# Graph network layer with a residual norm: the first edge layer's bias and maximum on VectorE, more rows fetched outside GpSimd

## What is computed

```python
ef = relu(edge_attr @ We1 + be1) @ We2 + be2          # edge_attr: 106250 x 64
ef = ef * sigmoid(edge_weight[:, None] @ Wt + bt)
msg = relu(concatenate([x[src], ef], axis=1) @ Wn1 + bn1) @ Wn2 + bn2
out = segment_sum(msg, dst, num_segments=6250)
return layernorm(x + (out + x))
```

## Time and profile before

| | us |
|---|---|
| median of 3 runs | 1045.51 (1045.18 to 1046.26) |
| the profiled execution, its own time | 1047.54 |
| its span in the trace | 1045.7 |
| PE busy | 850.5 (81%) |
| PEld busy | 613.4 (59%) |
| DVE busy | 650.3 (62%) |
| ACT busy | 492.0 (47%) |
| POOL busy | 777.1 (74%) |
| mean granted TensorE clock | 0.956 of full |

### The profile page before, as it was taken

The page is one execution under the profiler, slowest core; times in us unless marked ns, Lnnn a source line. Parts: engine busy times, 40 slices in busy tenths (PEclk is TensorE's granted clock), DMA queues, the critical chain, the costliest instruction groups (busy, mean ns, idle before and its releaser), DMA issues.

```text
span 1045.7 us, 21663 instructions
## 1 busy us (share of the span) xinstructions
PE 850.5 (81%) x5035; PEld 613.4 (59%) x5036; DVE 650.3 (62%) x1688; ACT 492.0 (47%) x668; POOL 777.1 (74%) x826
## 2 busy tenths in 40 slices
PE   6989998888788779787887777778888797887884
PEld 6766666566566556455555555555555565664653
DVE  4767775755665655656467466566566566566566
ACT  5565454445355445344445445444444444544432
POOL 7776777777777777777777777777777777777773
PEclk9999999999999998999899999998998998999997
DMA  8984555565554544554455445454544554554311
GB/s 231 284 232 121 146 146 147 145 155 144 145 154 123 153 141 126 134 154 138 123 145 154 137 124 156 116 145 130 158 128 124 145 145 127 143 144 145 84 53 49
DMA packets 158963, 148.85 MB, mean 142 GB/s; under 512 B 123255, under 2 KB 127414, under 8 KB 158822
## 3 DMA queue, kind: packets, MB, share of 16 engines
q1 hardware_dynamic: 128550, 89.86, 30.8%
q0 software_dynamic: 26144, 53.60, 19.5%
q10 hardware_dynamic: 4128, 3.87, 1.1%
HBM read 140.85 MB, written 6.40 MB: 141 GB/s over the span
## 4 chain that ended last, share of the span: by engine, by line
POOL 53%; issue 24%; PE 8%; DMA 7%; DVE 5%; ACT 2%; SPq 1%; DVEq 0%; ACTq 0%; POOLq 0%
POOL gathered L532 53%; DMA gathered<-node_table,src_e 5%; PE psS L852 2%; DVE h L1173 2%; PE psM L894 2%; DMA x_sb<-in_x 1%; PE psH L907 1%; PE psE L919 1%; ACT tw L693 1%; ACT h L625 0%; DVE onehot L1179 0%; SPq L431 0%; SPq L425 0%; PE psS L837 0%; DVE gathered L1047 0%
## 5 line engine op out<-in xcount | busy, mean ns | idle before, releaser
L532 POOL DMA_INDIRECT gathered<-node_table,src_e x785 | 745.2, 949 | 241.4 <-issue 233.9
L698 ACT ACTIVATE h<-psH,be_c 128x1024 f32<-128x1024 f32 x104 | 115.9, 1115 | 450.3 <-PE psH L907 450.3
L852 PE MATMUL psS<-onehot,h 128*128 128x128 f32 x1656 | 224.6, 291 | 63.0 <-ACT h L625 61.0
L1173 DVE TENSOR_TENSOR h<-psM,gathered 128x1024 f32<-128x1024 f32 (+1 forms) x104 | 122.6, 1182 | 222.8 <-DMA gathered<-node_table,src_e 184.6
L852 PEld LDWEIGHTS psS<-onehot,h 128*128 128x128 f32 x1656 | 207.6, 203 | 81.9 <-issue 41.4
L919 PE MATMUL psE<-h,we 128*128 128x512 f32 x416 | 218.4, 650 | 0.0
L894 PE MATMUL psM<-wn,efw 128*128 128x128 f32 x1664 | 206.8, 278 | 4.8 <-DVE h L1173 4.8
L894 PEld LDWEIGHTS psM<-wn,efw 128*128 128x128 f32 x1664 | 198.5, 195 | 5.6 <-DVE h L1173 5.6
L1194 DVE SCALAR_TENSOR_TENSOR efw<-psE,be_c,tw 128x1024 f32<-128x1024 f32 x104 | 133.2, 1281 | 109.4 <-PE psE L919 104.5
L907 PE MATMUL psH<-eaT,we 64*128 64x512 f32 x416 | 121.1, 660 | 74.0 <-DMA gathered<-node_table,src_e 73.7
L1179 DVE TENSOR_SCALAR onehot<-split_ids,dst_e 128x65 f32<-128x65 f32 x832 | 173.8, 271 | 0.0
(11 more groups left out here) (115 smaller groups left out, 343.0 us busy)
## 6 DMA issues: line engine op xcount, KB each, us to landing
ew<-in_edge_weight SPq DMA_DIRECT2D x104, 512.0 KB, 4.1
ea<-in_edge_attr SPq DMA_DIRECT2D x104, 256.0 KB
fetched<-node_table SPq DMA_DIRECT2D x1152, 0.5 KB
gathered<-node_table,src_e POOLq DMA_INDIRECT x785, 2.5
raw_own<-node_table ACTq DMA_DIRECT2D x768, 0.5 KB
x_sb<-in_x SPq DMA_DIRECT2D x6, 512.0 KB, 9.4
out_y<-x_sb ACTq DMA_DIRECT2D x12, 256.0 KB
node_table<-gathered SPq DMA_DIRECT2D x7, 256.0 KB, 5.2
```

Of the source, the lines that this page charges most:

```text
L532: pool.indirect_dma_start(to, None, rows, bass.IndirectOffsetOnAxis(index, 0)).then_inc(landed, by)
L698: nc.scalar.activation(h1[:, s % 2, :], psH[:, :, :].rearrange("p r e -> p (r e)"), ACT.Relu, bias=be1_c[:, :]).then_inc(h1_ready, 1)
L852: return nc.tensor.matmul(to, h[:, (k - SUM_LAG) % BODY * PAIR + q, t * C:(t + 1) * C], hot, start=(t == 0), stop=(t == TILES - 1))
L1173: return nc.vector.tensor_tensor(to, of, rows, ALU.add)
```

## The change

It does five things. (1) In steps from 4 on VectorE makes the first layer's bias and maximum (`first_layer`, a TENSOR_SCALAR from psH to h1, add then max) in place of ScalarE; in VectorE's program it stands after the counts and ahead of pre. TensorE waits for it before it writes psH again and before the second layer. (2) SP fetches 16 rows a step in eight steps, for twelve pairs (14, 22, ... 102); ScalarE 12 rows a step in eleven steps, for eight pairs (17, 28, 39, 50, 61, 72, 83, 95). ScalarE's rows land in memory of `dst_rows`. (3) The gathers of pairs 8 and 9 go to `raw_own`, free once pre of pairs 2 and 3 is done; later pairs use the four places of `gathered` shifted by two. `CLOSE_FROM` stays at 20. (4) In the last block the inverse root is found from a square root by ScalarE, a reciprocal and one correction (`end_scale`). (5) The staging of the last block's sums is split between VectorE and ScalarE.

The diff, cut:

```diff
+ROOT_BY = 8.0 / 3.0
...
-FETCH_ROWS, FETCH_STEPS = 13, 10
-FETCHED = list(range(17, 98, FETCH_STEPS))
-ACT_ROWS, ACT_STEPS, ACT_FROM = 8, 16, 6
-ACT_FETCHED = list(range(ACT_FROM + ACT_STEPS, 103, ACT_STEPS))
+SPARE = range(8, 10)
+FETCH_ROWS, FETCH_STEPS = 16, 8
+FETCHED = list(range(14, 103, FETCH_STEPS))
+ACT_ROWS, ACT_STEPS, ACT_FROM = 12, 11, 6
+ACT_FETCHED = [p + (p in FETCHED) for p in range(ACT_FROM + ACT_STEPS, 102, ACT_STEPS)]
...
-        act_fetched = raw_own[:, 0, 0:2 * C].rearrange("p (a c) -> p a c", c=C)
+        act_fetched = dst_rows[:, 0, 0:2 * C].bitcast(F32).rearrange("p (a c) -> p a c", c=C)
...
+        def rows_of(p):
+            if p in SPARE:
+                return raw_own[:, (p - SPARE.start) * PAIR:(p - SPARE.start + 1) * PAIR, :]
+            at = (p if p < SPARE.start else p - len(SPARE)) % BODY * PAIR
+            return gathered[:, at:at + PAIR, :]
...
+        def added_for(p):
+            if p >= CLOSE_FROM:
+                return p - 1
+            if p in SPARE:
+                return RAW_BEFORE // PAIR + p - SPARE.start + 1
+            return max(p - (BODY - 1) - (len(SPARE) if p < SPARE.stop + BODY else 0), 0)
...
+            for n in range(PAIRS, FETCHED[-1] + 4):
+                fetch_rows(n)
...
             for p in range(RAW // PAIR, PAIRS):
-                if p >= CLOSE_FROM:
-                    pool.wait_ge(pre_ready, p - 1)
-                    pool.nop(nofuse=True)
-                elif p >= RAW // PAIR + BODY:
-                    pool.wait_ge(pre_ready, p - (BODY - 1))
+                if p >= RAW // PAIR + BODY:
+                    pool.wait_ge(pre_ready, added_for(p))
                     pool.nop(nofuse=True)
...
                 if live(i, k, 0):
                     act.wait_ge(eaT_ps, s + 1)
+                    if s > BODY:
+                        act.wait_ge(h1_ps, s - 1)
                     nc.scalar.activation(eaT[:, k % 2, :], psT[:, :], ACT.Copy).then_inc(eaT_ready, 1)
...
-                    if s:
+                    if 0 < s < BODY:
                         relu_h1(s)
...
+                nc.scalar.activation(eps_root[:, :], eps_c[:, :], ACT.Sqrt)
+                act.wait_ge(acc_added, G)
+                stage_half(b)
+                act.wait_ge(full.moments_ready, b * BT + BT)
+                act.nop(nofuse=True)
+                nc.scalar.activation(half[:, :], mean_var[:, :, 1], ACT.Sqrt, bias=eps_c[:, :],
+                                     scale=ROOT_BY * ROOT_BY).then_inc(end_root, 1)
...
                     pe.wait_ge(eaT_ready, s + 1)
+                    if not raw:
+                        pe.wait_ge(h1_ready, s)
...
-                    if isinstance(i, int) and s - EF_LAG == PAIRS - 1:
-                        pe.wait_ge(h1_ready, PAIRS)
+                    if not raw:
+                        pe.wait_ge(h1_ready, s - EF_LAG + 1)
...
+            def first_layer(g, k):
+                dve.wait_ge(h1_ps, g + 1)
+                nc.vector.tensor_scalar(h1[:, k % 2, :], psH[:, :, :].rearrange("p r e -> p (r e)"), be1_c[:, :], 0.0,
+                                        ALU.add, ALU.max).then_inc(h1_ready, 1)
...
+                if live(i, k, 0) and not (isinstance(i, int) and s < BODY):
+                    first_layer(s, k)
                 if live(i, k, MSG_LAG):
                     pre(s - MSG_LAG, i, k)
...
+            def end_scale(b):
+                nc.vector.tensor_scalar(var[:, :], mean_var[:, :, 1], EPS, None, ALU.add).then_inc(end_step, 1)
+                dve.wait_ge(end_root, 1)
+                nc.vector.reciprocal(rstd[:, :], half[:, :]).then_inc(end_step, 1)
...
-                    scale(full, b, slice(0, BT + 1))
+                    end_scale(b)
```

More of the change, by code:

```diff
@@ L216, in gnn_kernel @@
         gather_in = [[sem(f"gather_in{i}_{part}") for part in range(2)] for i in range(BODY)]
+        spare_in = [[sem(f"spare_in{i}_{part}") for part in range(2)] for i in SPARE]
         rows_in = [sem(f"rows_in{i}") for i in range(2)]
@@ L346, in main_loop @@
                 held.update(before)
-                for k in range(BODY):
-                    step(1, k)
-                    finish(1, k)
+                for i in range(1, FIRST_TURN):
+                    for k in range(BODY):
+                        step(i, k)
+                        finish(i, k)
                 held.clear()
-                with eng.Fori(2, TURNS) as i:
+                with eng.Fori(FIRST_TURN, TURNS) as i:
                     for k in range(BODY):
@@ L728, in stage, with stage_half @@
                         .then_inc(staged, 1)
+            def stage_half(b):
+                nc.scalar.activation(staged_sums.rearrange("c (t p) -> c t p", t=BT)[:, BT // 2:BT, :],
+                                     sums[:, bass.ds(b * BN, BN)].rearrange("c (p t) -> c t p", t=BT)[:, BT // 2:BT, :],
+                                     ACT.Copy).then_inc(end_staged, 1)
             def finish(i, k):
@@ L970, in follow_gathers @@
                 if isinstance(p, int) and RAW // PAIR <= p < PAIRS - 1:
-                    pe.wait_ge(gather_in[p % BODY][part], p // BODY * (16 * PART[part]))
+                    landed, count = landing(p, part)
+                    pe.wait_ge(landed, count)
             def raw_transposes(n):
@@ L1209, in pre @@
                 else:
-                    rows = gathered[:, at, :]
+                    slot = (place - len(SPARE)) % BODY * PAIR
+                    rows = rows_of(g) if isinstance(g, int) else gathered[:, slot:slot + PAIR, :]
                     for part in range(2):
-                        dve.wait_ge(gather_in[place][part], (i - 1 if k < MSG_LAG else i) * (16 * PART[part]))
+                        landed, count = (landing(g, part) if isinstance(g, int)
+                                         else (gather_in[slot // PAIR][part], (i - 1) * (16 * PART[part])))
+                        dve.wait_ge(landed, count)
                 make_pre(h[:, at, :], psM[:, :, :], rows).then_inc(pre_ready, 1)
@@ L1441, in end @@
                     b = dve.snap(blocks, min_val=0, max_val=FULL - 1)
-                    stage_one(b, staged_sums, sums)
+                    nc.vector.tensor_copy(
+                        staged_sums.rearrange("c (t p) -> c t p", t=BT)[:, 0:BT // 2, :],
+                        sums[:, bass.ds(b * BN, BN)].rearrange("c (p t) -> c t p", t=BT)[:, 0:BT // 2, :])\
+                        .then_inc(staged, 1)
                     last_y()
```

35 lines of the change are left out of this document (29 added, 6 removed).

## The result

The changed kernel takes 1056.75 us, median of 6 runs (1054.89 to 1059.3), against 1047.04 us for the kernel before, 6 runs (1045.18 to 1048.04). The ratio is 1.0094, 95% interval [1.0081, 1.0107]: 9.7 us slower. The forecast was 5.2 us slower, 1050.7, with a range from 1042 to 1060. The sign and the main mechanism held; the measured change is nearly twice the forecast one.

The account below looks back on a forecast made before the run. GpSimd's gathers end to end were taken as the bound; -6.25 (gathers) - 1.95 (spare buffer) + 14.2 (wait at pair 20) + 0.5 (later waits) - 1.3 (end) = +5.2, so 1045.5 + 5.2 = 1050.7 us, range 1042 to 1060.

Parts of the forecast that it names:

- What bounds the kernel and where it waits: GpSimd's gathers, 1.25 us each, bound the kernel; from pair 20 they wait for pre of p-2, 6.1 us to spare.
- Gathers: GpSimd: five gathers fewer, 780 left, 5 x 1.25 = -6.25 us if GpSimd stays the bound.
- both streams cost nothing: SP's and ScalarE's longer fetches fit beside their other work in a step, so they add no time.
- rival 1: Delay never reaches GpSimd, change is faster: 1043 with a short instruction, 1036.0 with first layer off the loop; chance 0.17.
- SP: SP's 16 rows take 6.46 us after a 1.7 us gap; it keeps up with GpSimd, 0.65 us to spare.
- Spare buffer: GpSimd at pair 8: the gap at 85.67 shrinks from 2.26 to 0.3 us, -1.95 us.
- First layer: VectorE, ahead of pre: 1.14 us instruction, clean steps 7.3 to 8.46 us, GpSimd waits 14.2 us once at pair 20.
- The later waits: GpSimd after pair 20: further waits bounded by 0 and 1 us for each of 12 blocks; 0.5 us taken.
- Rival 2: After pair 20 the pipeline runs close behind and GpSimd waits again at blocks: 1062, or 1056 at half; chance 0.15.
- The end: Last block: shorter inverse root -1.0 us, split copy of sums -0.3, table load hidden; -1.3 us together.
- Rival 3: A fetch stream becomes the bound: SP up to 139 us, late rows of some pairs about 10 (1060); chance 0.04.
- Rival 4: The wait at pair 20 lands between the cases, gain and loss cancel: within 0.2% of before; chance 0.08.

Follow-up runs that it names:

- close_32: The changed kernel with CLOSE_FROM at 32 instead of 20, so GpSimd's tighter wait starts at pair 32; 1055.72 us.
- behind_pre: The changed kernel with VectorE making the first layer of a step behind pre of the pair two before instead of ahead of it; 1043.63 us.
- fetch_alone: The kernel before with only the new fetch lists (SP 16 rows a step, ScalarE 12), 780 gathers; 1044.77 us.
- rows_8: The changed kernel with ScalarE's old fetch list, 8 rows a step for a pair every 16 steps, 783 gathers; 1057.15 us.
- layer_alone: The kernel before with only the first layer moved to VectorE ahead of pre; lists, buffers and end as before; 1059.58 us against 1046.84.
- close_never: The changed kernel with CLOSE_FROM at 104 instead of 20, so GpSimd waits for pre of pair p-4 throughout; 1051.79 us.
- both: The changed kernel with first_layer behind pre on VectorE and CLOSE_FROM at 104; 1039.65 us, 0.993 of the kernel before.
- best: The kernel both, with ScalarE's fetches beginning at pair 17 instead of 6 and the last step's first_layer ahead of pre; 1038.69 us, 0.9923 of the kernel before.
- act_first: The changed kernel with the first layer back on ScalarE and all else kept; 1045.56 us.

## Why the prediction was right, and where it was not

**What bounds the kernel and where it waits.** Right. The step that decided the case, that the loop of the early steps sets pre of pair 18 and pre of pair 18 sets GpSimd, is what the trace shows: the gather of pair 20 starts 0.76 us after pre of pair 18 ends. close_32 confirms it by moving the place of the wait, and behind_pre shows that the place of the new instruction makes the lag.

**Gathers.** 780, at 1.25 us each, as said: -6.25. But "both streams cost nothing" was wrong. It summed ScalarE's work against the length of a step, where the question is what stands ahead of the relu in ScalarE's queue. The twelve rows take 4.6 to 5.1 us to issue (5.1 forecast), and in behind_pre and fetch_alone they end after pre. In the changed kernel the delay of pre itself covered nearly all of it in the early steps (the relu of step 12 comes 0.1 to 0.2 us later with twelve rows than with eight). What it cost there in all, rows_8 could not tell. What fell with it is the 1036.0 that rival 1 gives for a first layer off the loop altogether: behind_pre is that case, and took 1043.6.

**SP.** Right. The rows took 6.5 us (6.46 forecast) in most of the 96 steps, and the gap ahead of them was 1.39 to 1.46 us in most of them, at most 2.04:

```profile
179.20 0.43 SPq L476 DMA_DIRECT2D ea<-in_edge_attr  x1
181.05 6.50 SPq L537 DMA_DIRECT2D fetched<-node_table  x16
```

From the end of the load at 179.63 to the first row is 1.42 us, as in the fast one of the two gaps in the earlier trace rows. I had scaled it by the number of rows to 1.7, and it does not scale. The reading that the steps whose first row number is a multiple of four have the short gap held, as now all have it. (These are three of the ten steps of a fetch in the kernel before, not every fourth as I wrote.)

**Spare buffer.** -1.95 forecast, -1.96 measured. With the moved layer and without the spare buffer (layer_alone) the wait at pair 8 was 7.07 us. But what the buffer spares there is collected at pair 20, so the sum was right for the changed kernel.

**First layer.** The instruction: 1.14 forecast, 1.20 to the next one's start (1.28 long). Relu: 3.58 after psH forecast, 3.63 measured. The clean step: 8.46 against 8.50. The 16 early steps together: 144.2 forecast (194.6 - 67.99 + 17.6), 145.0 measured. psH of step 20: 212.2 against 212.78; end of pre of pair 18: 215.7 against 216.38. GpSimd was ready at 201.7 (201.5 forecast). The wait: 14.2 against 15.44. Of the 1.2 that this term is short, 0.6 is psH's place, and 0.76 the time from the end of pre to the first gather that it releases (217.14 - 216.38), a term that I left out and that stands in every wait of this kind. That the early steps agree to 0.8 us is in part luck: the same program took 143.3 and 141.6 us for them in close_never and close_32, and the step 12 of 10.76 us in the changed kernel's trace is one at a low clock.

**The later waits.** This is the step that failed: 0.5 forecast, 3.4 measured, 2.9 of the 5.3 us by which the sum missed the profiled execution. I set GpSimd's 9.75 us a pair against the clean step of 8.5 and concluded that the others draw level and keep 3 us to spare. The comparison had to be with their mean step, the long steps of the blocks in it: 9.63 us (close_never), and 9.69 from step 20 to 35 in the changed kernel. So they gain hardly anything on GpSimd. The trace shows it in what TensorE waits for ahead of psH, the sixth landed tile (changed kernel, then before):

```profile
PE psH L957 <- DMA gathered<-node_table,src_e: 24.9, 20, 2.6
```

```profile
PE psH L907 <- DMA gathered<-node_table,src_e: 73.7, 46, 3.7
```

A third of the waiting for tiles is left, and from pair 36 to 101 pre starts 5.1 us after the last gather of its pair on the mean, against 2.4 before. Rival 2 described this (running close behind, waits at blocks) at 6 to 12 us; 3.4 us came, in a few waits and not at every block. Of the two causes that it named, ScalarE's staging and a lower clock behind TensorE's idle time, both are seen in step 52 of close_never. But over the whole run the clock cost hardly more than before: the sums take 297 ns each instead of 291, psE 625 in place of 650, and the mean granted clock is 0.967 against 0.956. The groups, changed kernel and before:

```profile
L900 PE MATMUL psS<-onehot,h 128*128 128x128 f32 x1656 | 231.4, 297 | 121.6 <-ACT h L658 121.5
L969 PE MATMUL psE<-h,we 128*128 128x512 f32 x416 | 209.0, 625 | 0.0
```

```profile
L852 PE MATMUL psS<-onehot,h 128*128 128x128 f32 x1656 | 224.6, 291 | 63.0 <-ACT h L625 61.0
L919 PE MATMUL psE<-h,we 128*128 128x512 f32 x416 | 218.4, 650 | 0.0
```

**The rest of the ledger.** About 1.0 us, not in the sum. The page has 951 ns for a gather, against 949, which would give 1.5 us over 764 of them; what makes them longer stays open.

**The end.** -1.3 forecast, -1.14 measured. The timeline of VectorE and ScalarE:

```profile
1045.08 1.28 ACT L786 ACT_TABLE_LOAD   x1
...
1046.38 0.20 ACT L786 ACTIVATE eps_root<-eps_c 128x1 f32<-128x1 f32 x1
...
1046.76 0.67 ACT L767 ACTIVATE staged_own<-acc 128x256 f32 x1 [0.18 <-DVE acc L1185]
...
1046.94 0.39 DVE L1523 COPY staged_own<-acc 128x256 f32 x1 [0.33 <-DVE acc L1185]
...
1050.51 0.17 DVE L1458 TENSOR_SCALAR var<-mean_var 128x5 f32<-128x5 f32 x1
...
1051.99 0.17 DVE L1447 SCALAR_TENSOR_TENSOR shift<-mean_var,rstd 128x5 f32<-128x5 f32 x1
```

From var to the end of shift is 1.65 us (1.5 forecast) against 2.58: -0.93. The split gave nearly the rest. ScalarE's half takes 0.67 us, more than the 0.61 that the whole took VectorE, but TensorE starts on VectorE's half of 0.39 us and comes to ScalarE's later. From the last addition to the sums to var it is 4.11 us, against 4.34 before: -0.23, where -0.3 was forecast. (The last addition starts at 1046.40 and at 1034.77, TensorE's first product of the halves at 1047.48 and at 1036.08.)

The table load was hidden, as said. What the Trainium skill, ScalarE: Activation LUTs, section "What ACT_TABLE_LOAD costs", gives for a switch, 2.66 us with the drain, is not borne out here: the next activation starts 1.30 us after the load does, and the load itself starts 0.02 us after the relu ahead of it ends (1043.46 + 1.60). What a drain would do in another place no run here shows.

**The rivals.** Rival 1 fell in the changed kernel: the new instruction was 1.28 us long and on the loop. In behind_pre, where it lies off the loop, the kernel is faster, as rival 1 says. Rival 3 did not come in the changed kernel, where ScalarE never waited for fetched rows; in both and best, where the rest runs faster, it did wait for them. Rival 4 did not come.

**Open.** The tail differs by 1 to 2 us between kernels (14.5 in the changed kernel, 14.6 in close_32, 15.9 in behind_pre, 16.7 in act_first). That psH of the last pair waits behind pre in behind_pre is an argument from the program; best, which turns the order round in the last step alone, went from 16.5 to 15.3 and has another edit besides, so it is not shown apart.

## What to carry to other kernels

An instruction that waits for something late must not stand ahead of one on the same engine that is ready and on the loop: here the place cost 13 us, and the same work one place further back cost nothing that could be seen. Ask of every engine not whether its work fits into a step, but what is queued ahead of the instruction that the others wait for; ScalarE, 37% busy, was late through DMA issues that do not even count as busy. When two bounds are compared, take the mean step with the rare long ones in it. Keep the conditions for buffers loose while the followers still catch up: a wait that the bounding engine has made is lost, and with a loose condition and faster followers there was none (both). And do not read a difference of 2 us between two traces as the effect of an edit before an execution of the same program has been set beside it.

## What the runs showed of the hardware beyond that

The gap ahead of SP's fetched rows was in most cases the same 1.4 us for 13 rows in the kernel before and for 16 in the changed one, and 3.07 to 3.26 us in most of the steps of the kernel before that read 13 rows from a first number that is no multiple of four (up to 4.1 in a few). So at a multiple of four the count of 13 or 16 made no difference, and the place of the first number did. At the other places the count counts too: the last step of each fetch, with 11 rows, had 2.7 to 2.8 us. Why, no run here shows.

A gather that waited over 0.5 us for pre started 0.76 to 0.78 us after the end of that pre, in all 19 such waits of eight kernels. That is 0.47 us more than the ordinary gap.

TensorE's granted clock fell, in some steps, in or behind short idle times ahead of the sums: 1.89 us of idle time in step 12 of the changed kernel, 2.44 in step 8 of behind_pre, with sums of 3.63 and 3.50 us. In step 12 of close_32 it stayed at 1.00 over 1.80 us, with sums of 2.05 us.
